# Second FFN of a two-layer block: three result buffers in turn, and each tile's rows stored by themselves

## The reference

```python
router_logits = jnp.einsum('sbh,eh->sbe', hidden_states, router_w)
routing_indices = jnp.argmax(router_logits, axis=-1)
out = jnp.zeros_like(hidden_states)
for e in range(E):
    mask = (routing_indices == e)[..., None]
    xe = jnp.where(mask, hidden_states, 0.0)
    g = jnp.einsum('sbh,ih->sbi', xe, gate_w[e])
    u = jnp.einsum('sbh,ih->sbi', xe, up_w[e])
    ye = jnp.einsum('sbi,hi->sbh', jax.nn.silu(g) * u, down_w[e])
    out = out + jnp.where(mask, ye, 0.0)
...
x = x + jnp.tanh(g_ffn[1]) * _L1_ffn_ref(_layernorm(x, axis=-1), ...)
```

## Time and profile before

| | us |
|---|---|
| median of 3 runs | 825.15 (824.63 to 825.51) |
| the profiled execution, its own time | 822.23 |
| its span, first to last instruction | 820.5 |
| second FFN, first scatter issued to last scatter issued | 729.6 to 814.7 |
| busy over the whole span: PE, DVE, ACT, POOL | 94%, 75%, 67%, 57% |
| 39 scatters of line 1880, each on POOL | 0.98 to 1.02 |

### The profile page before, as it was taken

How to read it: one execution, slowest core, us unless ns; L and a number is a source line. 1 busy time by engine, 2 the same in 40 slices (tenths; PEclk the granted TensorE clock), 3 DMA queues, 4 the chain that set the end, 5 groups by cost and what they waited for, 6 DMA issues and landing times. The chain is left out here.

```text
span 820.5 us, 30377 instructions
## 1 busy us (share of the span) xinstructions
PE 771.0 (94%) x10574; PEld 632.3 (77%) x10579; DVE 616.2 (75%) x2394; ACT 548.7 (67%) x1109; POOL 469.1 (57%) x876
## 2 busy tenths in 40 slices
PE   4999999998999989999999999999999998888895
PEld 2777777776788868888888888888888886367774
DVE  5899999998777767888888887878888787434442
ACT  2687888786555568777777777777777774155652
POOL 6555777772011265767667767667767674224444
PEclk9999999999999999999999999999999999999998
DMA  8805999500200000000000000000000000122000
GB/s 230 293 2 173 276 258 242 128 1 3 71 1 0 0 2 2 3 7 7 7 7 0 7 7 7 7 7 0 7 7 7 7 7 5 41 73 63 25 29 18
DMA packets 56160, 41.69 MB, mean 51 GB/s; under 512 B 3897, under 2 KB 51651, under 8 KB 55856
## 3 DMA queue, kind: packets, MB, share of 16 engines
q1 hardware_dynamic: 52400, 36.39, 16.8%
q0 software_dynamic: 2272, 4.27, 1.6%
q10 hardware_dynamic: 1440, 0.40, 0.3%
HBM read 18.07 MB, written 23.44 MB: 51 GB/s over the span
## 5 line engine op out<-in xcount | busy, mean ns | idle before, releaser
L1678 PE MATMUL l_pv<-l_Z,l_probs 128*128 128x129 f32 x1024 | 164.4, 284 | 3.0 <-ACT l_probs L1506 1.4
L1678 PEld LDWEIGHTS l_pv<-l_Z,l_probs 128*128 128x128 f32 x1024 | 138.3, 191 | 21.8 <-issue 5.2
L1439 POOL TENSOR_TENSOR l_qk_lo<-w,l_qk_hi 128x512 f16<-128x512 f32 x128 | 144.5, 1159 | 0.6 <-ACT l_qk_hi L1500 0.4
L1161 DVE SCALAR_TENSOR_TENSOR x_sb<-l_pv,l_inv,x_sb 128x128 f32 (+1 forms) x256 | 89.8, 351 | 33.7 <-DVE l_inv L1148 6.5
L1496 ACT ACTIVATE w<-l_qk_bank 128x512 f32<-128x512 f32 x124 | 74.1, 597 | 53.3 <-PE l_qk_bank L52 51.6
L52 PE MATMUL l_tz<-M,cT 128*128 128x512 f16 x384 | 104.1, 380 | 0.5 <-ACT l_Z L1511 0.3
L1506 ACT ACTIVATE l_probs<-l_b 128x512 f32<-128x512 f32 x128 | 72.7, 594 | 44.4 <-PE l_b L1644 44.2
L520 DVE TENSOR_REDUCE n_shared<-fold_bank 128x4 f32<-128x512 f32 x128 | 87.4, 684 | 9.5 <-PE fold_bank L735 9.3
L1138 DVE TENSOR_REDUCE l_neg_max<-l_a 128x4 f32<-128x512 f32 x128 | 83.2, 681 | 2.2 <-PE l_a L1622 2.1
L1500 ACT ACTIVATE l_qk_hi<-w 128x512 f16<-128x512 f32 x124 | 77.4, 624 | 1.1
L1511 ACT ACTIVATE l_Z<-l_tz 128x512 f32<-128x512 f32 x124 | 74.1, 597 | 4.9 <-PE l_tz L52 1.4
(11 more groups left out here) (291 smaller groups left out, 2287.6 us busy)
## 6 DMA issues: line engine op xcount, KB each, us to landing
expert_rows<-empty_row SPq DMA_DIRECT2D x8, 2178.0 KB, 23.6
x_sb<-expert_rows SPq DMA_DIRECT2D x36, 66.0 KB, 2.4
x_sb<-in_x SPq DMA_DIRECT2D x4, 512.0 KB, 6.5
ctx_sb<-in_ctx SPq DMA_DIRECT2D x4, 512.0 KB, 7.7
w<-in_L_ffn_w SPq DMA_DIRECT2D x1, 2048.0 KB, 9.2
w_raw<-in_L_ffn_gate_w SPq DMA_DIRECT2D x1, 1408.0 KB, 9.9
w_raw<-in_L_ffn_up_w SPq DMA_DIRECT2D x1, 1408.0 KB, 12.0
downT<-in_L_ffn_down_w SPq DMA_DIRECT2D x2, 512.0 KB, 4.0
```

The source lines that it names most:

```text
L1161: nc.vector.scalar_tensor_tensor(out=total, in0=O[:, h, 0:P], scalar=inv[:, j:j + 1], in1=total, op0=ALU.mult, op1=ALU.add).then_inc(summe ...
L1439: nc.gpsimd.tensor_tensor(qk_lo[:, w, m, Q * u:Q * u + Q].rearrange("p t n -> p (t n)"), qk[:, u, m, :], qk_hi[:, w, m, Q * u:Q * u + Q].r ...
L1678: last = nc.tensor.matmul(pv_bank[m % 2][:, h * (P + 1):(h + 1) * (P + 1)], probs[:, 2 * m + h, :], Z[:, w, 2 * m + h, :], start=True, sto ...
```

## The change

Results and tokens get three buffers in turn instead of two, each with a semaphore of its own, and POOL waits for one result before each scatter in every step, as it did before in the last one only.

```diff
@@ second_ffn
+    RESULTS = 3
-        result = sb("result", [P, 2, U, P])
+        result = sb("result", [P, RESULTS, U, P])
-        token = sb("token", [P, 2, U], mybir.dt.uint32)
+        token = sb("token", [P, RESULTS, U], mybir.dt.uint32)
...
-                def results(i, v, half_i, p):
+                def results(i, v):
+                    p = i % RESULTS
                     if v == 0:
-                        if not isinstance(half_i, int) or half_i:
-                            dve.wait_ge(stored[p], 16 * U * half_i)
+                        if i >= RESULTS:
+                            dve.wait_ge(stored[p], 16 * U * (i // RESULTS))
...
-                def scatter(i, p):
-
-                    last = isinstance(i, int) and i == STEPS - 1
+                def scatter(i):
+
+                    p = i % RESULTS
                     pool.wait_ge(token_ready, i + 1)
                     for v in range(U):
-                        if v == 0 or last:
-                            pool.wait_ge(result_ready, U * i + (v + 1 if last else U))
+                        pool.wait_ge(result_ready, U * i + v + 1)
                         if v == 0:
                             pool.wait_ge(taker_ready, i + 1)
                             nc.gpsimd.tensor_tensor(taker[:, 1:2], ...).then_inc(taker_ready, 1)
...
-                for p in range(2):
-                    pool.wait_ge(stored[p], 16 * U * ((STEPS + 1 - p) // 2))
+                for p in range(RESULTS):
+                    pool.wait_ge(stored[p], 16 * U * len(range(p, STEPS, RESULTS)))
```

More of the change, by code:

```diff
@@ L1797, in second_ffn @@
         names = ("zeroed taker_ready hn_ready T_moved T_hi_ready T_lo_ready gate_done up_done "
-                 "silu_ready hid_ready hidT_moved hidT_ready down_done token_ready result_ready stored_even stored_odd").split()
+                 "silu_ready hid_ready hidT_moved hidT_ready down_done token_ready result_ready stored_0 stored_1 stored_2").split()
         (zeroed, taker_ready, hn_ready, T_moved, T_hi_ready, T_lo_ready, gate_done, up_done,
-         silu_ready, hid_ready, hidT_moved, hidT_ready, down_done, token_ready, result_ready, stored_even, stored_odd) = map(sem, names)
-        stored = (stored_even, stored_odd)
+         silu_ready, hid_ready, hidT_moved, hidT_ready, down_done, token_ready, result_ready, *stored) = map(sem, names)
         def row(n, first=0, end=P):
@@ L1856, in step @@
                         if v < 2 and live(-1):
-                            results(i - 1, v + 1, half_i - 1 + p, 1 - p)
+                            results(i - 1, v + 1)
                         if v == 2 and live(0):
-                            results(i, 0, half_i, p)
+                            results(i, 0)
                 for v in range(U):
@@ L1884, in step @@
                     if live(-1):
-                        scatter(i - 1, 1 - p)
+                        scatter(i - 1)
                 every_step(pool, step)
-                for p in range(2):
-                    pool.wait_ge(stored[p], 16 * U * ((STEPS + 1 - p) // 2))
+                for p in range(RESULTS):
+                    pool.wait_ge(stored[p], 16 * U * len(range(p, STEPS, RESULTS)))
             @block.scalar
```

## The result

The changed kernel takes 810.01 us in the median (809.07 to 811.92, 4 runs) against 824.89 (824.01 to 825.51, 4 runs) beside it: a ratio of 0.9827, 95% interval 0.9809 to 0.9846. The forecast was 815.3 with a range of 813.5 to 825.0. The profiled execution took 811.92 us with a span of 810.2 (822.23 and 820.5 before).

A forecast was written before the change was run, and what follows sets the result against it. PE was taken to bound the second FFN, its reports delayed by bursts of three scatters, with queued scatters at the end. Steps -8.1 and end -1.7 gave -9.8: 815.3 us from a median of 825.15, range 813.5 to 825.0.

The forecast's parts named there:

- Third buffer 0: DVE's wait before the token cast: relaxing it gains 0, since the cast already starts with no idle time before it.
- The end -1.7: Last step: its third scatter starts at 813.02 instead of 814.73, no longer held up by the previous step's burst; -1.7 us.
- Single scatters hold nothing: Second FFN steps: scatters about 2.1 us apart leave PE's reports alone, like a burst's first scatter, harmless up to 0.29 after its end.
- x: Time after a scatter's end for which PE's reports stay held; up to 0.30 us it costs nothing.
- the ring: Result, scatter and next PE report wait on each other; a step takes 5.42 + 3x or 6.32, whichever is longer.
- B: Rival, half: in the steps each scatter holds reports for x = 0.45; steps 6.77, time 818.6; chance 0.14.
- D: Rival, slower: each scatter holds reports long, x = 0.83 (for it, a second-attention report 1.05 late); steps 7.91, 830.0; chance 0.16.
- The steps -8.1: Ten steps of the second FFN, from 7.26 to 6.45 us each by single scatters: -8.1 us, at most -9.4.
- the quiet step: Second FFN step from 724.03, before any group of three scatters: 6.32 us, PE busy 6.18; taken as lower bound.
- A: The forecast: single scatters leave PE's reports alone, steps of 6.32 to 6.6, time 814.0 to 817; chance 0.48.
- C: Rival, only the end gains: steps stay at 7.26, the end gives 1.7, time 823.4; chance 0.22.
- What would show it: Profile signs: scatters about 2.1 apart, 0.30 behind a result; steps 6.3 to 6.6; PE's wait for results under 2 us.

The follow-up runs named there:

- the spread kernels: Three buffers, burst after the third result, with a POOL memset between scatters: 2.0 us apart 814.89 (ratio 0.9917), 1.6 us apart 812.02 (0.9883).
- The burst kernel: Three buffers with the burst of three scatters, against that kernel started one result later: 813.90 (ratio 1.0021) on chip B, 824.86 (1.0046) on chip C.

## Where the prediction was right, and the step that failed

**The cause: right, and shown.** The prediction took the late reports for an effect of three scatters in a burst. Spreading the same scatters takes the lateness away (7.17 to 6.30 on chip A, 7.20 to 6.21 on C), leaving the burst and adding the buffer doesn't. What the trace of before could not show is the condition: on chip B bursts cost nothing.

**Third buffer 0: right.** 0.9990 with it alone, and single stores with two buffers have steps of 6.23 as against 6.22.

**The end -1.7: right**, -1.72.

**Single scatters hold nothing: right.** The nearest row, a first scatter's end 0.29 ahead of a report, was the one to go by. In the semaphore times of the changed kernel's trace five down products' reports just behind a scatter are 0.04 to 0.14 late up to 753.4, inside the slack of 0.41; they come 0.32 to 0.36 after the scatter's end, a little over the 0.30 from which x would cost something if every report of a step were held. It is one of three in a step, and from 754 on none is over 0.02 late, so the ring of rivals B and D never closes. D's row, 1.05 us from the end of a pair's first scatter to the report's arrival, was a row of a pair and not of a single one.

**The steps -8.1: the step that failed.** Both halves of it were wrong in the same direction. 6.32 was called the lower bound of the step, but the quiet step is no floor: it is 6.32 with PE busy for 6.18 of it, in the earlier trace rows itself, and it is 6.31 to 6.39 in every profile here, with any kind of store. It has gaps of its own (0.14 here, 0.18 in the changed kernel), where the later steps have 0.00 to 0.12, 0.04 in the mean. When nothing is held, they take 6.17 to 6.30 in turn. And on top of that floor came 0.13 for doubt. So 6.45 should have been 6.22: ten steps × 0.23 = 2.3 us, which is all of the difference between -9.8 and the -12.07 of the traces.

**From the profile to the median: the other one.** The prediction carried the difference between two profiled executions over to the median. The median of before was 2.7 above its profiled execution (824.89 and 822.23), the median of the changed kernel 1.9 below its own. -12.07 on 824.89 is 812.8; measured is 810.0. This rest of 2.8 us has no place in a trace: what lies ahead of the second FFN varies between executions (its first products start between 714.7 and 719.6 over the profiles of all kernels here), and the other sets of runs with held steps gave -10.9 (A, two buffers) and -11.6 (D). I can't say why the result gave -14.9; its ratio makes it -14.3, with an interval of -12.7 to -15.8. The range's low end of 813.5 was the false floor (825.15 - 9.4 - 1.7 = 814.05) with 0.5 us for such a spread: what the traces show of the stage would have put the time at 813.1 (825.15 - 12.07), already below it.

**The rivals.** A held, beyond its better end. B and D fell with x. C, only the end gains, fell wherever the steps of before are held, but chip B is its picture, for a reason that the prediction had not seen: there, before has no loss in its steps to give back. Its share of the evidence, that in the earlier trace rows a report is prompt behind a second scatter, was read rightly as a row that speaks against "always", and it is still unexplained: at before's end six scatters follow each other by 1.29 to 1.37, from 808.17 to 814.73, and PE's reports of 808.78, 809.11 and 812.33 are all 0.01 late. The rule that C leaned on, from the Trainium skill, "SBUF — State Buffer", section "Who interferes with whom", says that PE and ACT never wait on anyone. Of execution the trace agrees: PE's products in a held step are as long as ever (0.83 for six). But the report of a finished product was up to 1.3 us late at its consumer, and by that PE lost 0.9 a step. A rule on who slows whom doesn't cover when others learn of it.

**What would show it.** Scatters 1.82 and 2.40 apart, 2.1 in the mean; 0.28 behind a result; steps of 6.17 to 6.30 (forecast 6.3 to 6.6); PE's wait for results 1.4 (under 2). The last sentence of the list named a hold that depends on how much PE does, and not on how the scatters follow each other. That the scatters' distance counts is shown, since the spread kernels leave PE the same work. Whether PE's work counts as well is open: the end of before, where PE has little more than one down product at a time and nothing is held, suggests that it does, and no kernel here tests it. The other condition, the chip, wasn't on the list.

## What to carry to other kernels

Compare the end of each producer with the start of its idle consumer; where the two are further apart than usual (0.04 us here), look at what another engine issues in just that time, and spread indirect DMAs over the step rather than bursting them (where they held anything, 1.6 us from start to start was enough and 1.3 was not). Take the floor of a step from the busy time of the engine that bounds it, not from the length of the best step seen, and let the range go below it. Where a gain rests on an effect between engines, time both kernels on more than one chip: here the changed kernel gained 1.7%, 1.4% and 0.2% in three sets of runs.

## What the chips showed that was not expected

- **A hold that depends on the chip.** The kernel before: 812.08 on chip B, 820.89 to 824.89 in the four other sets of runs. The burst kernel, one program, has steps of 6.25 on B and 7.19 on C. The changed kernel takes nearly the same in its three sets of runs: 810.0 to 812.4. The profiles of B differ in one more thing: they have 8438 to 8463 semaphore updates on record, the thirteen others 7703 to 7888, for nearly the same instructions. Why chip B holds nothing, and whether the two go together, is open.
- **Held reports come out in a row.** In the semaphore times of before's step of the earlier trace rows, four reports of PE, of work that ended at 740.07, 740.51, 740.96 and 741.29, arrive at 741.378, .429, .480 and .531: 0.05 apart. The reports of ACT and DVE that the trace has for the steps are prompt (0.01). It looks like a queue of PE's reports that stands still and then drains; the runs show the lateness, not the queue.
- **Writing the rows doesn't matter.** With no row written the scatters take POOL as long (three in 3.6 us), and the hold is the same.
- **A long memset on POOL slows DVE, but not always.** With a memset of 128x768 (0.77 us), the token cast takes 1.50 for 0.16 and the result behind it about 1.07 for 0.35 in every step that has memsets, both until the first memset's end; a result beside the step's second memset takes 0.35. With 128x256 (0.34 us) the cast takes 0.39 and every result 0.35. Why the first one is slow and the second isn't, these runs don't show.
